# A scan layer with a mixture of experts, one core: dt by way of its eight sums per token, and grams beside the y products

## The reference

```python
x = x + attn(layernorm(x)); x = x + ffn(layernorm(x))
# attn: proj = rmsnorm(h) @ w_in_proj, split into z, x, B, C and dt_raw (8 columns)
dt_raw = proj[..., o4:]
x = silu(conv4(x))
dt = softplus(dt_raw @ w_dt + b_dt)                 # w_dt: 8 x 256
dt_h = dt.reshape(Bz, S, N_HEADS, HEAD_DIM).mean(-1)
# ssd_scan, for each chunk:
lcs = jnp.cumsum(dt_c * A, axis=1)
M = jnp.exp(jnp.where(mask, lcsT[..., :, None] - lcsT[..., None, :], -jnp.inf))
G = jnp.einsum('blhn,bihn->bhli', C_c, B_c)          # the gram
intra = jnp.einsum('bhli,bihp->blhp', M * G, x_c)
inter = jnp.einsum('blh,blhn,bhpn->blhp', jnp.exp(lcs), C_c, h)
h_new = total_decay * h + jnp.einsum('bhl,blhp,blhn->bhpn', M[:, :, -1, :], x_c, B_c)
# then y * silu(z), rmsnorm, out projection, residual
# ffn: relu(x @ w1) @ w2 for 2 + 4 experts, hidden size 512
```

## Time and profile before

| | |
|---|---|
| median of 3 runs | 564.11 us (564.02 to 567.18) |
| the profiled execution, its own time | 563.96 us |
| its span, first to last instruction | 562.2 us, 11668 instructions |
| busy: TensorE matmuls | 541.9 us (96%) |
| busy: VectorE, ScalarE, GpSimd | 443.7 us (79%), 352.4 us (63%), 173.6 us (31%) |
| TensorE's granted clock, mean | 0.998 of full speed |

### The profile page before, as it was taken

One profiled execution on the slowest core, in us unless ns is written; L12 is line 12 of the kernel. 1 busy time (PEld: TensorE's weight loads), 2 busy tenths in 40 slices (PEclk: granted clock), 3 DMA queues, 4 the chain that ended last, 5 costly groups with the idle time before them and its releaser, 6 DMA issues.

```text
span 562.2 us, 11668 instructions
## 1 busy us (share of the span) xinstructions
PE 541.9 (96%) x3912; PEld 427.8 (76%) x3912; DVE 443.7 (79%) x1044; ACT 352.4 (63%) x760; POOL 173.6 (31%) x232
## 2 busy tenths in 40 slices
PE   8887989999999999999999999999999999999996
PEld 7666768878787777877787777778777787877774
DVE  4888878978889787878888788887888788775654
ACT  3884689547774578636776387745886377752442
POOL 3074016520162203620154201722055211532010
PEclk9999999999999999999999999999999999999999
DMA  6650036100560007200380005600162004400120
GB/s 202 186 144 22 1 91 163 59 1 2 159 170 1 2 6 225 101 1 0 117 189 21 0 0 175 151 0 0 41 209 76 0 0 143 169 2 1 33 67 19
DMA packets 37354, 41.41 MB, mean 74 GB/s; under 512 B 3483, under 2 KB 27717, under 8 KB 37317
## 3 DMA queue, kind: packets, MB, share of 16 engines
q1 hardware_dynamic: 36724, 40.80, 25.3%
q10 hardware_dynamic: 592, 0.15, 0.1%
HBM read 37.79 MB, written 3.15 MB: 73 GB/s over the span
## 4 chain that ended last, share of the span: by engine, by line
PE 60%; DVE 21%; ACT 8%; issue 7%; DMA 2%; POOL 2%; DVEq 0%; ACTq 0%; SPq 0%; POOLq 0%
PE bank L426 9%; PE bank L428 6%; PE bank L427 6%; PE bank L536 6%; PE bank L641 5%; PE bank L642 5%; PE bank L643 5%; DVE cv L1122 4%; DVE act_l L1273 4%; PE bank L548 3%; ACT act_h L873 3%; PE bank L564 2%; PE bank L522 2%; DVE dsum L1138 2%; PE bank L558 2%
## 5 line engine op out<-in xcount | busy, mean ns | idle before, releaser
L1273 DVE SCALAR_TENSOR_TENSOR act_l<-bank,act_h 128x512 fp32r<-128x512 f32 x192 | 131.6, 687 | 51.5 <-ACT act_h L873 49.4
L873 ACT ACTIVATE act_h<-bank 128x512 fp32r<-128x512 f32 x192 | 114.6, 597 | 84.9 <-PE bank L428 81.3
L1496 POOL TENSOR_TENSOR late<-late 128x512 f32<-128x512 f32 x31 | 39.8, 1285 | 167.2 <-DVE late L1281 166.7
L426 PE MATMUL bank<-fTl,w1h 128*128 128x512 f32 x192 | 87.1, 453 | 3.0 <-DVE act_l L1273 2.0
L893 ACT ACTIVATE seg<-seg,lneg 128x128 f32<-128x128 f32 x256 | 81.2, 393 | 1.5 <-DMA seg<-lc_rows 1.5
L641 PE MATMUL bank<-act_l,w2h 128*128 128x512 f32 x192 | 77.6, 404 | 1.5 <-DVE act_l L1273 1.5
L642 PE MATMUL bank<-act_h,w2l 128*128 128x512 f32 x192 | 76.0, 396 | 0.0
L428 PE MATMUL bank<-fTh,w1h 128*128 128x512 f32 x192 | 75.7, 394 | 0.0
L643 PE MATMUL bank<-act_h,w2h 128*128 128x512 f32 x192 | 75.5, 393 | 0.0
L427 PE MATMUL bank<-fTh,w1l 128*128 128x512 f32 x192 | 75.5, 393 | 0.0
L1483 POOL TENSOR_TENSOR xw<-xs,seg 128x128 f32<-128x128 f32 x48 | 20.2, 422 | 132.2 <-ACT seg L893 70.9
(11 more groups left out here) (177 smaller groups left out, 1058.9 us busy)
## 6 DMA issues: line engine op xcount, KB each, us to landing
seg<-lc_rows SPq DMA_DIRECT2D x32, 512.0 KB, 3.8
late<-gk_rows SPq DMA_DIRECT2D x8, 1024.0 KB, 8.8
grow<-lc_rows SPq DMA_DIRECT2D x48, 128.0 KB, 4.9
x_in<-L_attn_hidden_dram SPq DMA_DIRECT2D x8, 256.0 KB, 3.0
out_dram<-late SPq DMA_DIRECT2D x8, 256.0 KB, 5.3
late<-L_ffn_sw_dram SPq DMA_DIRECT2D x2, 512.0 KB, 6.4
late<-L_ffn_rw_dram SPq DMA_DIRECT2D x1, 1024.0 KB, 7.3
CT<-L_attn_w_in_proj_dram SPq DMA_DIRECT2D x1, 512.0 KB, 5.5
```

Of the source, the lines that this page charges most:

```text
L426: mm(dst, stat_h, mov_l, start=True, stop=False)
L873: nc.scalar.activation(act_h[:, b % RING, :], HID[b % 2][:], ACT.Relu).then_inc(act_h_ready, 1)
L1273: v_.scalar_tensor_tensor(act_l[:, r, :], HID[b % 2][:], 0.0, f(act_h[:, r, :]), ALU.max, ALU.subtract)\
```

## The change

**dt.** The product of w_dt with the eight columns is gone. In its place TensorE makes the eight sums dt_raw of each token (`dt_sums`, two matmuls of 512 columns into the transposes' bank), laid out three times in 128 rows together with their low halves. ScalarE copies all of it (`z_copy`), VectorE makes the low part in 16 rows (`z_low`), and one matmul of 256 columns for each chunk multiplies it by a table that holds the high and low halves of w_dt; four matmuls in place of twelve in slot 2. For the next sequence the sums are made in slot 22, ahead of its `proj` 0. w_dt is loaded six times by SyncE into a zeroed tile instead of once by ScalarE. In the opening the projections' order is 0 to 5, and `proj` 2 and 3 wait for the table and the sums.

**Scan.** From sequence 1 on the gram of chunk c+1 is made in slot 14+3c, right ahead of the y product of chunk c; the state product moves from slot 14+3c to 13+3c; VectorE makes the new state in slot 13+3c and the masked grams of chunks 1 to 3 in slots 15, 18 and 21: the first half ahead of `act_low`, the second half behind it (in slot 21 both ahead). `norm1` is cut in two, and `norm1_apply` stands behind the second masked half. In sequence 0 the grams, states and masks stay in their places.

```diff
-        w_dt = sb("w_dt", [NH, DI])
-        wdt_col = sb("wdt_col", [P, NH])
-        wdtT = sb("wdtT", [NH, P])
+
+        wz_all = sb("wz_all", [P, P], F32R)
+        wz_high = sb("wz_high", [P, P], F32R)
+        wdt_raw = sb("wdt_raw", [P, DI])
+        wdt = sb("wdt", [P, DI], F32R)
+        zT = sb("zT", [P, SEQ], F32R)
...
+            sp_eng.wait_ge(zeros_set, 5)
+            for r in (0, 8, 32, 40, 64, 72):
+                sp_eng.dma_start(wdt_raw[r:r + NH, :], a["w_dt"]).then_inc(wdt_in, 16)
...
+                if j in (2, 3):
+                    pe.wait_ge(z_ready, nth(s, 1, 1))
...
-                        ins = split(dst[:, k * DI:(k + 1) * DI], hTh[:, at(c)], hTl[:, at(c)], wh[:, DT0:DT0 + DI], wl[:, DT0:DT0 + DI])
+                        ins = mm(dst[:, k * DI:(k + 1) * DI], zT[:, at(c)], wdt[:], start=True, stop=True)
...
+            def dt_sums(s):
+                if is_seq(s, 0):
+                    pe.wait_ge(wz_set, 3)
+                pe.wait_ge(hTl_ready, nth(s, 1, 1))
+                mm(TR[:], wz_all[:], hTh[:], start=True, stop=False)
+                mm(TR[:], wz_high[:], hTl[:], start=False, stop=True).then_inc(z_psum, 1)
...
-            def y_product(s, c):
-
+            def state_product(s, c):
                 if c > 0:
                     pe.wait_ge(state_step, nth(s, 8, (2, 5, 8)[c - 1]))
-                if c < NCH - 1:
-                    pe.wait_ge(btok_ready, nth(s, 3, c + 1))
-                    pe.wait_ge(xw_ready, nth(s, 6, 2 * c + 2))
-                    for n in range(NP):
-                        ins = mm(MAIN[1][:, n * 64:(n + 1) * 64], btok[:, at(n)], xw[:, n, :, :].rearrange("p t d -> p (t d)"),
-                                 start=True, stop=True)
-                    ins.then_inc(s_psum, 1)
+                pe.wait_ge(btok_ready, nth(s, 3, c + 1))
+                pe.wait_ge(xw_ready, nth(s, 6, 2 * c + 2))
+                for n in range(NP):
+                    ins = mm(MAIN[1][:, n * 64:(n + 1) * 64], btok[:, at(n)], xw[:, n, :, :].rearrange("p t d -> p (t d)"),
+                             start=True, stop=True)
+                ins.then_inc(s_psum, 1)
+
+            def y_product(s, c):
+
+                if c == NCH - 1:
+                    pe.wait_ge(state_step, nth(s, 8, 8))
+                if c < NCH - 1 and not is_seq(s, 0):
+                    gram(s, c + 1, None)
                 if c > 0:
                     pe.wait_ge(y_steps, nth(s, 8, 2 * c))
...
-                    if b == 0:
+                    if b == 0 and (c == NCH - 1 or is_seq(s, 0)):
...
-                    if step == 1:
+                    if step == 1 and c == 0:
                         gram(s, c, prev)
-                        if c == NCH - 1 and not is_seq(s, n_seq - 1):
-                            proj(s + 1, 0)
+                    if step == 1 and c < NCH - 1:
+                        state_product(s, c)
+                    if step == 1 and c == NCH - 1 and not is_seq(s, n_seq - 1):
+                        dt_sums(s + 1)
+                        proj(s + 1, 0)
                     if step == 2:
...
-                keep_busy_early(10)
-                pe.wait_ge(wdt_col_set, 1)
-                nc.tensor.transpose(MAIN[1][0:NH, 0:P], wdt_col[:], ident[:]).then_inc(wdtT_psum, 1)
-                pe.wait_ge(wdtT_set, 1)
-                pe.wait_ge(wdt_in, 16)
-                mm(MAIN[2][:, 0:DI], wdtT[:], w_dt[:], start=True, stop=True).then_inc(wdt_psum, 1)
-                keep_busy_early(8)
+                keep_busy_early(14)
                 hn_transposes(0)
                 pe.wait_ge(rows_in, 6 * 16)
-                nc.tensor.transpose(MAIN[0][:, 0:34], rows[:], ident[0:34, 0:34]).then_inc(cols_psum, 1)
-                keep_busy_early(5)
-                for j in (2, 3, 0, 1, 4, 5):
+                nc.tensor.transpose(MAIN[3][:, 0:34], rows[:], ident[0:34, 0:34]).then_inc(cols_psum, 1)
+                keep_busy_early(4)
+                dt_sums(0)
+                for j in range(6):
...
+            def z_copy(s):
+                act.wait_ge(z_psum, nth(s, 1, 1))
+                nc.scalar.copy(zT[:], TR[:]).then_inc(z_high_ready, 1)
...
+                act.wait_ge(zeros_set, 7)
+                for t in (wz_all, wz_high):
+                    nc.scalar.activation(t[:, 0:96].rearrange("p (k q) -> p k q", q=32)[:, :, 0:NH],
+                                         w_raw[:, 1536:1544].unsqueeze(1).to_broadcast([P, 3, NH]), ACT.Identity, scale=wn_in[:]).then_inc(wz_set, 1)
...
+                z_copy(0)
+                act.wait_ge(wdt_in, 6 * 16)
+                nc.scalar.copy(wdt[:], wdt_raw[:]).then_inc(wdt_set, 1)
...
+            def norm1_stats(s):
                 dve.wait_ge(x_loaded, nth(s, 16, 16))
                 for c in range(NCH):
                     v_.bn_stats(st1[:, c, :], x_in[:, c, :]).then_inc(ln1_stats, 1)
+
+            def norm1(s):
...
+            def z_low(s):
+                dve.wait_ge(z_high_ready, nth(s, 1, 1))
+                v_.tensor_tensor(zT[32:48, :], TR[32:48, :], f(zT[32:48, :]), ALU.subtract).then_inc(z_ready, 1)
...
+            def masked_gram(s, c, hf):
+                dve.wait_ge(g_psum, nth(s, 8, 2 * c + hf + 1))
+                dve.wait_ge(decay_masked, nth(s, 8, 2 * c + hf + 1))
+                if hf == 0 and (v := nth(s, 4, c)) is not None:
+                    dve.wait_ge(y_psum, v)
+                v_.tensor_tensor(mg[:, hf], MAIN[2 + hf][:].rearrange("p (n l) -> p n l", n=NP), decay(c)[:, hf], ALU.mult)\
+                    .then_inc(mg_ready, 1)
+
             def attend(s, c, step):
-                if step == 1:
-                    for hf in range(2):
-                        dve.wait_ge(g_psum, nth(s, 8, 2 * c + hf + 1))
-                        dve.wait_ge(decay_masked, nth(s, 8, 2 * c + hf + 1))
-                        if hf == 0 and (v := nth(s, 4, c)) is not None:
-                            dve.wait_ge(y_psum, v)
-                        v_.tensor_tensor(mg[:, hf], MAIN[2 + hf][:].rearrange("p (n l) -> p n l", n=NP), decay(c)[:, hf], ALU.mult)\
-                            .then_inc(mg_ready, 1)
+                if step == 1 and (c == 0 or is_seq(s, 0)):
+                    masked_gram(s, c, 0)
+                    masked_gram(s, c, 1)
...
+            def next_state(s, c):
+                first = (0, 2, 5)[c]
+                if c > 0:
+                    dve.wait_ge(grow_ready, nth(s, 3, c))
+                    v_.tensor_tensor(state_m[:], state[:, (c - 1) % 2], grow[:, c % 2, :, P - 1:P].to_broadcast([P, NP, 2 * HD]),
+                                     ALU.mult).then_inc(state_step, 1)
+                    dve.wait_ge(state_step, nth(s, 8, first + 1))
+                    first += 1
+                dve.wait_ge(s_psum, nth(s, 3, c + 1))
...
+                        if i in (15, 18, 21):
+                            masked_gram(s, i // 3 - 4, 0)
+                        if i == 15 and not is_seq(s, n_seq - 1):
+                            norm1_stats(s + 1)
+                        if i == 21:
+                            masked_gram(s, 3, 1)
...
+                    if s is not None and i == NBLK - 4 and not is_seq(s, n_seq - 1):
+                        hT_low(s + 1)
+                    if s is not None and i == NBLK - 2 and not is_seq(s, n_seq - 1):
+                        z_low(s + 1)
...
+                    if s is not None and i in (15, 18):
+                        masked_gram(s, i // 3 - 4, 1)
+                    if s is not None and i in (13, 16, 19):
+                        next_state(s, i // 3 - 4)
+                    if s is not None and i == 15 and not is_seq(s, n_seq - 1):
+                        norm1(s + 1)
+                    if s is not None and i == 18 and not is_seq(s, n_seq - 1):
+                        norm1_apply(s + 1)
```

91 lines of the change are left out of this document (47 added, 44 removed).

## The result

| | before | changed |
|---|---|---|
| median of 14 runs | 564.48 us (563.92 to 567.18) | 567.99 us (567.02 to 569.48) |
| ratio | | 1.0057 (95% interval 1.0044 to 1.0069) |
| the profiled execution's span | 562.2 us | 566.3 us |

The changed kernel is 0.6% slower. The forecast was 563.2 us with a range to 567.5: the wrong direction, and 0.5 us outside.

What follows compares the result with a forecast made beforehand. TensorE, 96% busy, was taken as the bound, with a VectorE chain at the turns. 563.96 + 0.8 + 0.46 - 0.56 - 0.90 - 0.61 = 563.15, plus 0.15 to the median: 563.2 us, range 559.2 to 567.5.

Steps and rivals of the forecast that it cites:

- VectorE from slot 17 on: Slots 17 to 22: VectorE fills its idle time, slot 22's low half comes about 0.2 us late, TensorE loses zero.
- Grams beside y: Slots 14, 17, 20: putting gram ahead of y saves TensorE 0.205 us per merge, 0.61 a sequence, in seven sequences.
- The fourth rival: Merges give nothing because both edges move to the state product's new place; 567.5 us, chance 0.04.
- The third: Rival: gram to y costs no step, so each merge gives 0.1 us more; 560.9 us, chance 0.13.
- Sequence 7, -0.61: Last sequence: it makes no sums for another, so it keeps the merges' whole gain of 0.61 us.
- GpSimd's weighing: Sign the forecast is wrong: the state product, a slot earlier, stalls for its inputs weighed on GpSimd; no size given.
- Slot 2's saving at zero: Sequences 2 to 7: the dt projection's 0.93 us less on TensorE becomes waiting for `act_low`, gaining nothing.
- the sums' 0.46: `dt_sums` costs TensorE 0.46 us in slot 22 of sequences 1 to 6 and once at the opening's end.
- the opening: Before the first scan: dt waits for sums, `z_copy` and `z_low`, ready at 13.6 to 14 us; +0.8 us, excluding sums.
- Sequence 1's slot 2: VectorE waits there for TensorE's dt, so fewer dt matmuls win 0.56 us.
- The first rival: Slot 2's dt saving counts at the turns, 5.6 us more gained; 557.6 us, chance 0.12.
- The second: Rival: `z_low` makes VectorE late and the turn begins about 0.5 us late in six sequences; 566.2 us, chance 0.20.

Runs made afterwards that it cites:

- e3: The changed kernel with the low part of the sums (`z_low`) made for only 8 of 512 columns; 566.97 us, ratio 1.0038.
- e14: The changed kernel with slot 21's second masked half behind the low half, the first staying ahead of the expert sum; 567.17 us, ratio 1.0040.
- e5: The changed kernel with each of slot 2's four dt matmuls made three times from sequence 1 on; 568.26 us, ratio 1.0061.
- e2: The kernel before with the new dt alone, the scan's order as before; 568.87 us, ratio 1.0067.
- e13: The changed kernel with three of the next sequence's conv taps behind the last low half and one behind the mean square; 577.92 us, ratio 1.0231.
- e9: The changed kernel with two of the next sequence's conv taps moved behind the last low half and two behind the mean square; 566.60 us, ratio 1.0033.
- e16: The kernel before with the scan's new order, slot 21's second mask behind the low half, and conv taps placed as in e13; 567.23 us, ratio 1.0039.
- e1: The kernel before with the scan's new order alone, dt as before; 564.09 us, ratio 0.9981.
- e6: The changed kernel with chunk 0's state product and new state back in slot 14, ahead of gram and y; 567.62 us, ratio 1.0047.
- e8: The changed kernel with slot 3's projection (`proj` 4) moved into slot 2 ahead of the waiting block; 566.37 us, ratio 1.0016.
- e7: The changed kernel with the sums' low part made by GpSimd from an extra full-precision ScalarE copy; 572.24 us, ratio 1.0120.

## Why the prediction was wrong

By its own steps. The profiled pair's spans are 4.12 us apart and the sum had said -0.81, so 4.9 us are to be found: 1.4 in the merges, 1.1 at the turns, 0.8 in sequence 7, 0.9 in sequence 2's late transfer, 0.4 behind the last scan, and 0.3 in small terms.

- **The step that failed: "this isn't passed on: zero", of VectorE from slot 17 on.** The first half of its working held to a tenth: VectorE ran packed, the 0.76 us of idle time were used up and slot 22's low half came 0.2 late (its high half was there at 310.86 + 0.60 = 311.46, it began at 311.67). What failed is whom I asked about it. I asked TensorE, who wants that block two slots later. Behind it on VectorE stand two taps, y and the last low half without a pause, and TensorE wanted that one at once, already in the kernel before (0.64 where 0.23 is undisturbed and 0.40 the least that any run reached). Price by e3: 0.18 in each of six turns, 1.1 us.
- **"Grams beside y", -0.205 per merge**, was right in kind and too large: 0.14, in every run. The rest is the edge behind the state product (0.32 in place of 0.23), whose new place I had written down as one that "needs no such last step": the step went (0.12 less), but an edge came (0.09 more), which leaves 0.03 of the 0.095 that I had put there. (0.205 - 0.14) x 3 x 7 = 1.4 us. The fourth rival, that the edges move there, holds for a third of it. The third, gram to y free, is out: 1.09 us.
- **Sequence 7, -0.61, was +0.47.** I treated slot 21's two masks ahead of the expert sum as a matter of y alone. Without `dt_sums` and `proj` 0 behind it the expert sum's lateness is bare: from the last matmul of the `first` ahead of it to that `second` it is 1.00 (504.42 to 505.42), 0.77 over the undisturbed 0.23. e14 gives 0.35 of it back.
- **Sequence 2's late transfer**: 0.9 us in the profiled execution. The forecast named such a wait as what would make it wrong ("GpSimd's weighing ... late for the state product a slot earlier"), and gave it no price.
- **Slot 2's saving at zero** held (e5), and so did the sums' 0.46 (0.47 in e2) and the opening (+1.39 against +1.26; dt on VectorE at 13.83 us, forecast 13.6 to 14). Sequence 1's slot 2 was better than forecast, 0.86 against 0.56 (the rest of that body lost 0.5 again).
- **Slips without weight:** from the first to the last of the twelve dt matmuls are eleven distances, of which the first is 0.23; the other ten are the 0.117 that the forecast used. The wait that was to grow "from 0.35" is 0.23 by its own numbers (320.02 - 319.67 - 0.116), which gives 1.2 with the 0.93; 1.01 was measured.

The first rival was ruled out rightly. The second was given 0.20, with a criterion (12.1 us left, 12.2 needed; 12.0 left by the forecast's own 296.8 and 308.8) that came out on its side. A term whose own criterion says "exceeded" should not have stood in the sum at zero. What stays open: how the 3.5 us between the medians divide, since the late transfer is in some executions only, and the 0.44 us behind the last scan.

## What to carry to other kernels

When an engine's idle time is used up, don't ask who wants the next result: follow that engine's queue to the first result that somebody already waits for, and charge the lateness there. Work taken from the busiest engine is worth nothing where it waits for a chain beside it; make that a run (do the removed work anyway) before building on it. And an item moved into a wait has two more bills to read first: what the engine waited for may slow down beside it, and its queue may hold something that feeds on what was pushed back.

## What the hardware showed that I had not expected

**VectorE and GpSimd stop each other, and the stops chain.** A conv tap (L1160) reads two tiles from SBUF. In e13 the one that begins at 388.60 takes 1.65 us, alone it takes 0.75. The operation that runs when it begins is GpSimd's add (388.43 + 1.27 = 389.70), and the tap ends 0.55 us after that add. The root on GpSimd begins at 389.65, while the tap still runs, takes 1.47 us in place of 1.02, and ends 0.88 us after the tap. In e9 the first tap begins only 0.31 us before the add's end and takes 0.86, but the two distances are the same, 0.55 and 0.88, and its second tap, with the root alone beside it, takes 0.75 as ever. The two distances are the same in every turn of e9 to e13 and e16 that has a tap there, 36 in all: add holds tap, tap holds root. The Trainium skill, page "SBUF — State Buffer", has the reason in its "Terms" and "Summary: rules for kernel authors": VectorE and GpSimd share a pair of ports, an operation of VectorE with two SBUF inputs and one of GpSimd that reads SBUF exclude each other, and the one that comes second waits. The trace agrees where the tap meets the add and where the root meets the tap. It doesn't agree for e9's second tap: it comes second to the root, which reads SBUF too, and isn't held. There the measurement decides: the root doesn't keep the ports for the whole of its row.

**After a longer idle time the clock sometimes fell.** In e13 TensorE idles about 1 us more in slot 2 than in the changed kernel, in two pieces, 0.95 us ahead of the dt matmuls and 1.02 behind them, and in two of its turns, to sequences 5 and 7, the granted clock then fell. In the turns at 258 and 391 us the same two pieces stand and it stayed at 1.00; in the other 17 profiled executions, the changed kernel's with its 1.01 us among them, it fell at no turn. TensorE in 2 us windows, the turn to sequence 5 (the columns are window, length, busy us and instructions, granted clock, DMA share and GB/s):

```profile
324.00:326.00 2.00, 0.78 (x5) 1.00 0.00 0
326.00:328.00 2.00, 1.25 (x4) 0.80 0.00 0
328.00:330.00 2.00, 2.00 (x7) 0.50 0.00 0
330.00:332.00 2.00, 2.00 (x11) 0.84 0.00 0
```

0.50 is 1.2 of 2.4 GHz; that body took 67.50 us where its neighbours took 65.93, so 1.6 us for one such fall. The same was seen in sequence 0's scan, between 47 and 52.4 us, in five of the 18 profiled executions (e1, e2, e6, e8, e13; e2: 0.85 over 40 to 50 us; the kernels before and changed: 1.00), and once at 16 us (e7). In e1 the clock also rose late at the start: it was at 2.4 GHz from 11.4 us on, in the kernel before from 6.8, and VectorE's first `hTl` began at 13.02 us in place of 11.05. Falls and rises of this kind are worth 1 to 2 us each, as much as most differences here: e1's runs lie in two heaps, 561.9 to 563.5 and 564.7 to 567.0. That is likely why e1's interval holds 1 although its period is 0.35 us shorter; that the heaps are the clock's is not shown run by run.
